# Stage two of a graph kernel: ten blocks gathered at its beginning in place of three, then four blocks of adds with no gather between them

## What is computed

```python
h = relu(layernorm(x))
# layer 0: messages go from dst to src
gate = silu(edge_attr @ W1.T + b1) @ W2.T + b2 + adapt_logit(types of src and dst)
msg  = gate * h[dst] * (cutoff(distance) * mult[dst])
agg  = segment_sum(msg, src) / clip(segment_sum(mult[dst], src), 1e-8)
x    = x + layernorm(h + agg) * gamma + beta
# layer 1: messages go from src to dst
h    = relu(layernorm(x))
msg  = (relu(h @ weight1 + bias1) @ weight2)[src, rel_type] * norm
x    = x + relu(segment_sum(msg, dst) + bias2)
```

## Time and profile before

| | |
|---|---|
| time, median of 3 executions | 1542.93 us (1542.01 to 1545.06) |
| the profiled execution | 1533.91 us |
| its span, first to last instruction | 1532.2 us |
| busy: PE, DVE, ACT, POOL | 1157.1, 1336.7, 618.2, 1025.5 us |
| mean granted TensorE clock | 0.598 of full speed |

### The profile page before, as it was taken

How to read it: one execution, slowest core, us unless ns; L and a number is a source line. 1 busy time by engine, 2 the same in 40 slices (tenths; PEclk the granted TensorE clock), 3 DMA queues, 4 the chain that set the end, 5 groups by cost and what they waited for, 6 DMA issues and landing times.

```text
span 1532.2 us, 20105 instructions
## 1 busy us (share of the span) xinstructions
PE 1157.1 (76%) x5198; PEld 846.7 (55%) x5198; DVE 1336.7 (87%) x3937; ACT 618.2 (40%) x1423; POOL 1025.5 (67%) x809
## 2 busy tenths in 40 slices
PE   5898999989999989991047878888888888886000
PEld 2677777777777777771035555555555555554000
DVE  6999999999999999880299999999999999993598
ACT  2544444544445444440034444444444444442000
POOL 7655567777887676666537887887878878866100
PEclk9756555655556565555556565555655655557555
DMA  7999986666666566642446665555555555533899
GB/s 228 305 320 333 325 228 155 153 145 145 142 164 154 136 155 138 147 103 11 130 156 169 170 161 139 140 139 140 138 137 139 140 141 139 140 71 58 295 396 390
DMA packets 154389, 268.72 MB, mean 175 GB/s; under 512 B 73818, under 2 KB 90411, under 8 KB 153380
## 3 DMA queue, kind: packets, MB, share of 16 engines
q1 hardware_dynamic: 78228, 223.53, 43.5%
q0 software_dynamic: 68992, 24.64, 17.5%
q10 hardware_dynamic: 7056, 19.27, 3.1%
HBM read 194.33 MB, written 112.55 MB: 200 GB/s over the span
## 4 chain that ended last, share of the span: by engine, by line
PE 32%; DMA 20%; DVE 19%; POOL 15%; issue 11%; ACT 3%; SPq 1%; POOLq 0%; ACTq 0%; DVEq 0%
POOL agg L468 11%; PE ps_m L555 11%; DMA t<-agg,src_all 6%; PE ps_m L644 6%; PE ps_qs L555 4%; DMA agg<-x,once 3%; PE ps_k L630 3%; DMA lows<-low 2%; DVE x L1038 2%; DVE same L834 2%; DMA agg<-y,once 2%; DVE t L1042 2%; POOL nodes L426 2%; DMA agg<-ysq,once 2%; POOL agg L504 2%
## 5 line engine op out<-in xcount | busy, mean ns | idle before, releaser
L504 POOL DMA_INDIRECT agg<-sums,once x196 | 317.8, 1621 | 89.5 <-issue 64.1
L426 POOL DMA_INDIRECT nodes<-in_table,dst_all x196 | 194.1, 990 | 104.0 <-issue 50.2
L495 POOL DMA_INDIRECT t<-agg,src_all x196 | 190.3, 971 | 83.7 <-issue 49.1
L555 PEld LDWEIGHTS ps_m<-msg,same 128*128 128x128 f32 x980 | 200.4, 314 | 29.8 <-issue 29.8
L555 PE MATMUL ps_m<-msg,same 128*128 128x48 f32 x980 | 208.2, 398 | 1.0 <-issue 1.0
L630 PE MATMUL ps_k<-h_t,rw_sb 56*128 56x256 f32 x588 | 132.3, 571 | 96.3 <-ACT hid L724 73.7
L555 PEld LDWEIGHTS ps_qs<-msg,same 128*128 128x128 f32 x980 | 183.0, 288 | 2.1 <-DVE msg L926 2.1
L555 PE MATMUL ps_qs<-msg,same 128*128 128x49 f32 x980 | 180.1, 362 | 2.0 <-DVE msg L926 2.0
L468 POOL DMA_INDIRECT agg<-x,once x84 | 135.1, 1609 | 49.0 <-issue 21.9
L630 PEld LDWEIGHTS ps_k<-h_t,rw_sb 56*128 56x128 f32 x588 | 67.6, 260 | 144.6 <-ACT hid L724 100.6
L644 PE MATMUL ps_m<-hid,rw_sb 128*64 128x256 f32 x588 | 136.1, 634 | 0.0
(11 more groups left out here) (149 smaller groups left out, 2575.1 us busy)
## 6 DMA issues: line engine op xcount, KB each, us to landing
agg<-in_both SPq DMA_DIRECT2D x14, 2758.0 KB
t<-agg SPq DMA_DIRECT2D x49, 784.0 KB, 4.4
kept<-kept_out SPq DMA_DIRECT2D x49, 404.0 KB, 2.8
kept_in<-kept SPq DMA_DIRECT2D x49, 404.0 KB
agg<-bias_rows SPq DMA_DIRECT2D x49, 384.0 KB
out<-t ACTq DMA_DIRECT2D x49, 384.0 KB, 5.8
rows<-in_src_rows SPq DMA_DIRECT2D x49, 256.0 KB, 4.1
rows<-in_dst_rows SPq DMA_DIRECT2D x49, 256.0 KB, 3.2
```

The lines of the kernel that those rows point to most:

```text
L426: pool.indirect_dma_start(nodes[s][:, t, :], None, table, bass.IndirectOffsetOnAxis(ap=dst_all[:, c:c + 1], axis=0)).then_inc(nodes_in[b % ...
L495: pool.indirect_dma_start(t2[b % T2S][:, t, :], None, wide, bass.IndirectOffsetOnAxis(ap=src_all[:, c:c + 1], axis=0)).then_inc(ends_in[b ...
L504: pool.indirect_dma_start(agg1, bass.IndirectOffsetOnAxis(ap=once1[b % LAG1][:, t:t + 1], axis=0), sums1[b % LAG1][:, t, :], None, compute ...
L555: last = mm(ps[:, t * width:(t + 1) * width], kept_same[:, at:at + P], m[:, v, :], start=(v == t), stop=(v == TILES - 1))
```

## The change

A second kind of slot is made: `t2_early`, seven of them (`EXTRA` = `PRE1` - `T2S` = 10 - 3), lies in the beginning of `x_res`. Blocks 0 to 6 use these; block b from 7 on uses `t2[(b - 7) % 3]`. The semaphores `chunk_in` and `ends_in` become rings of ten. GpSimd gathers blocks 0 to 9 first, with no wait for an `x2_done` between them; the loop after them gathers block b + 6 only where that is 10 or more, so that the adds of blocks 0 to 3 stand alone. SP still loads chunks three blocks ahead. Both SP and GpSimd now wait for `agg1_set` before they write into slots, since the fills read `bias_rows`, which lies in the memory that `x_res` takes over; GpSimd had this wait ahead of its first add.

```diff
+PRE1 = 10
+EXTRA = PRE1 - T2S
...
+        x_flat = x_res[:, :, :].rearrange("p r h -> p (r h)")
+        t2_early = [x_flat[:, k * G * XW:(k + 1) * G * XW].rearrange("p (r w) -> p r w", w=XW) for k in range(EXTRA)]
+        def t2_slot(b):
+            return b if b < EXTRA else EXTRA + (b - EXTRA) % T2S
+        def t2_uses(b):
+            return 1 if b < EXTRA else (b - EXTRA) // T2S + 1
+        def t2_of(b):
+            return t2_early[b] if b < EXTRA else t2[(b - EXTRA) % T2S]
...
-        chunk_in = ring_of(sem, T2S, "chunk_in")
-        ends_in = ring_of(sem, T2S, "ends_in")
+        chunk_in = ring_of(sem, PRE1, "chunk_in")
+        ends_in = ring_of(sem, PRE1, "ends_in")
...
+            sp.wait_ge(S["agg1_set"], 16 * (NBLOCK + 1))
...
-                if t == 0:
+                if t == 0 and b >= PRE1:
                     need(pool, S["x2_done"], b - T2S + 1)
...
-            for b in range(AHEAD1):
+            pool.wait_ge(S["agg1_set"], 16 * (NBLOCK + 1))
+            for b in range(PRE1):
                 for t in range(TILES):
                     gather_wide(b, t)
-            pool.wait_ge(S["agg1_set"], 16 * (NBLOCK + 1))
             for b in range(NBLOCK):
                 for t in range(TILES):
                     add1(b, t)
-                if b + AHEAD1 < NBLOCK:
+                if PRE1 <= b + AHEAD1 < NBLOCK:
                     for t in range(TILES):
                         gather_wide(b + AHEAD1, t)
```

More of the change, by code:

```diff
@@ L215, in build @@
         x_res = sb("x_res", [P, RES * NR + TILES, H])
+        x_flat = x_res[:, :, :].rearrange("p r h -> p (r h)")
+        t2_early = [x_flat[:, k * G * XW:(k + 1) * G * XW].rearrange("p (r w) -> p r w", w=XW) for k in range(EXTRA)]
+        assert EXTRA * G * XW <= (NBLOCK - PRE1 - T2S) * NR * H
+        def t2_slot(b):
[4 more added lines that the diff above has]
+            return t2_early[b] if b < EXTRA else t2[(b - EXTRA) % T2S]
         def x_rows(b):
@@ L371, in load_chunk @@
                 need(sp, S["x2_done"], b - T2S + 1)
-                sp.dma_start(t2[s][:, TILES:G, :].rearrange("p r w -> p (r w)"), wide_chunks[b]).then_inc(chunk_in[s], 16)
+                sp.dma_start(t2_of(b)[:, TILES:G, :].rearrange("p r w -> p (r w)"), wide_chunks[b]).then_inc(chunk_in[t2_slot(b)], 16)
                 sp.dma_start(kept_in[s][:, TILES * H:TILES * H + KEPT], kept[b]).then_inc(kept_got[s], 16)
@@ L492, in gather_wide @@
                 c = b * TILES + t
-                if t == 0:
+                if t == 0 and b >= PRE1:
                     need(pool, S["x2_done"], b - T2S + 1)
-                pool.indirect_dma_start(t2[b % T2S][:, t, :], None, wide,
-                                        bass.IndirectOffsetOnAxis(ap=src_all[:, c:c + 1], axis=0)).then_inc(ends_in[b % T2S], 16)
+                pool.indirect_dma_start(t2_of(b)[:, t, :], None, wide,
+                                        bass.IndirectOffsetOnAxis(ap=src_all[:, c:c + 1], axis=0)).then_inc(ends_in[t2_slot(b)], 16)
             def add1(b, t):
@@ L933, in _ @@
                 yes = 0 <= b < NBLOCK
-                on = t2[b % T2S]
-                on_a = t2[a % T2S]
+                on = t2_of(b) if yes else None
+                on_a = t2_of(a) if a < NBLOCK else None
                 kin = kept_in[b % T2S]
@@ L938, in _ @@
                 if yes:
-                    dve.wait_ge(chunk_in[b % T2S], 16 * uses(b, T2S))
+                    dve.wait_ge(chunk_in[t2_slot(b)], 16 * t2_uses(b))
                     V.tensor_scalar(tot[:, :], on[:, :, XW - 1:XW].rearrange("p r o -> p (r o)"), 1e-8, None, ALU.max).then_inc(S["tot_done"], 1)
                 if a < NBLOCK:
-                    dve.wait_ge(ends_in[a % T2S], 16 * TILES * uses(a, T2S))
+                    dve.wait_ge(ends_in[t2_slot(a)], 16 * TILES * t2_uses(a))
                     V.tensor_reduce(asum[:, :], on_a[:, 0:TILES, 0:H], AX_X, ALU.add).then_inc(S["asum_done"], 1)
```

## The result

The changed kernel is slower. Its median is **1556.62 us** (1553.38 to 1559.27, 5 executions) beside 1542.93 us (1535.13 to 1546.87, 5) of the kernel before: a ratio of **1.0089**, 95% interval 1.0055 to 1.0123. Forecast were 1539.9 us and a range from 1536.0 to 1543.0, so the time lies outside it, on the other side of no change.

The account below looks back on a forecast made before the run. Stage two was taken as bound by a loop of copy, adds, gathers and `asum`, 26.00 us per two blocks. The only gain, 3.06 us at block 10, gave 1542.93 - 3.06 = 1539.9 us, range 1536.0 to 1543.0.

Parts of the forecast that it names:

- Forty gathers in a run: Start of stage two on POOL: 28 more gathers at 1.25 us end 9.7 us before the first add, costing nothing.
- Contention: Early stage two: extra gathers start after the first chunks land and delay only small later traffic with room; no cost.
- The stall of block 6: Stage two, block 6: its gathers land early, so `asum` no longer waits and comes 2.30 us earlier.
- Passes with adds alone: Stage two, blocks 7 to 9: gathers already in, 12.46 us per VectorE pass; lead grows to 3.06 us.
- Rival 2: Adds hold VectorE's `tot` in four free passes, 0.29 us each; gain only 1.9 us, 1541.0 us; chance 14%.
- What is late next: Block 10's gathers stand behind block 4's adds: `asum` waits about 1.1 us, yet comes 3.06 us earlier than before.
- The 16 gathers taken out of the loop: Blocks 6 to 9: POOL is spared 20.0 us, mostly not gained because adds wait for ScalarE's copies.
- the end of stage two: VectorE's schedule, not POOL's backlog, sets the end, so the 3.06 us lead reaches stage three whole.
- Rival 3: POOL alone is the limit in stage two: up to 20 us gained, 1522.9 us, or 1536 in small form; chance 8%.
- Waits on `agg1_set`: Before slot writes: fills issued 70 us earlier, so the waits are met and cost under 0.1 us each.
- Rival 4: POOL's queue stalls the forty gathers, each further one waiting for the previous landing: 11 us later, 1553.9 us; chance 6%.
- The bound of 0.2%: Whole kernel: 3.1 us taken as the smallest difference a measurement can tell from no change; forecast gain almost exactly there.

Follow-up runs that it names:

- e5: Kernel with the change but six blocks gathered early, plus 16 gathers nobody reads, so again forty in a run: 1551.87 us, ratio 1.0075 to the kernel before.
- e6: Kernel with the change but six blocks gathered early, plus 16 POOL memsets in place of further gathers: 1547.71 us, ratio 1.0023 to the kernel before.
- e7: Kernel before with gathers of block b + 6 put ahead of adds of block b in stage two's loop: 1527.82 us, ratio 0.9909.
- e9: Changed kernel with a small POOL memset, waited for, behind each of the 28 further gathers: 1530.24 us, ratio 0.9984 to the kernel before.
- e1: Kernel before, unchanged, run again for a second trace: 1543.80 us, a single execution.
- e8: Kernel before with two blocks instead of four gathered ahead at the start of stage one: 1535.45 us, ratio 0.9968.
- e3: Changed kernel with eight blocks gathered ahead instead of ten, a run of 32 gathers: 1549.91 us, ratio 1.0044 to the kernel before.
- e12: Changed kernel with further gathers paced by VectorE's progress, gathers ahead of adds, and two first blocks in stage one: 1518.58 us, ratio 0.9913 to the kernel before.
- e4: Changed kernel where, from block 3, a block's early gathers wait until those of the block before have landed: 1549.20 us, ratio 1.0051 to the kernel before.

## Why the prediction was wrong

- *Forty gathers in a run*: **the step that failed.** Its sum was right as far as it went. The run took 1.25 us each and lasted 50.4 us, from 753.18 to 803.60; without stage one's loss it would have ended at 794.3, and 793.7 were forecast. But "costs nothing" looked only at when POOL is wanted next. The price was on the engines beside it: 15.4 us in the changed kernel's trace. That the run of gathers makes it is shown by e5, which has the run but not the order of the change, against e6. It is not paid everywhere: nothing like it is in the traces of the third chip, where the changed kernel itself was not run.
- *Contention* failed with it. It counted bytes and the DMA engines' time, and there it was right: their share was 0.55 and not higher. The delay is not there.
- *The stall of block 6*: right. No wait of `asum` between blocks 2 and 9.
- *Passes with adds alone*: right, 12.46 to 12.60 us where 12.46 were forecast. *Rival 2* is in the difference: `tot` took 0.44 us at 841.12 and 853.72, and both passes took 12.60. It had 0.29 us for each of four passes; 0.14 in two of them was measured. The same mechanism, and not POOL's backlog, is most of what e7 has left above 12.46 us.
- *What is late next*: right in size, 3.06 us. The changed kernel gained 3.7 us after its stall and e9 3.6, or 2.6 each if e1 stands for the kernel before. Only the wait of 1.1 us at block 10 was not seen: its `asum` followed 12.52 us after that of block 9 in the changed kernel.
- *The 16 gathers taken out of the loop* and *the end of stage two*: right, the pace of later passes did not improve (13.03 against 12.97). *Rival 3* did not occur. The adds of block 44 were to start at about 1372. They started at 1398.21, again after a wait of 6.51 us for ScalarE's copy as in the earlier trace rows, so VectorE's schedule set the end, only 23.2 us later, carried from the two places above.
- *Waits on `agg1_set`*: right. The first gather waited 2.0 us for the last add of stage one, as before (1.99 us in the earlier trace rows).
- *Rival 4* had the right sign, the right part of the change and nearly the right size (11 us; 11.7 at block 10 by the traces), but another mechanism: a gather that waits for the one before it. POOL's pace never changed. What I held against it, was read one-sidedly: 32 gathers 1.30 us apart say that POOL can issue them so, and nothing of what the other engines do meanwhile. That execution showed no loss there, and the next one of the same kernel did (e1); the second condition was met in the one and not in the other. A question to one execution can't show what only some have; the 9 us between its time and the median were the hint, and I moved them over as a constant.
- *The bound of 0.2%* was too fine: with five executions of each kernel the interval of the ratio is 0.34% wide to either side, so that a gain of 3.06 us could not have been told from none.

**What stays open.** Which resource delays the others is not known. It is not the DMA engines' share (0.55, like before) and not POOL's being busy (e6). It is hardly the loading of instructions, with one packet of 0.02 MB for it between 778 and 803 us of the changed kernel, and two with as much in the same stretch of before. Most of the late starts are late semaphore updates, as shown above, but not all: `DVE_READ_ACCUMULATOR`, which waits for no semaphore and otherwise starts without a pause, started 0.42 us late at 805.72. Nor is the second condition known. All timed executions are recorded, and it is the record itself that has holes where losses occur. Between 778 and 808 us of the changed kernel 51 updates were due: 2 are recorded in time, 12 late and 37 not at all. So the recording, or whatever both share, is a rival that no run here excludes: it may be that the records and the gathers get in each other's way, and that the stall is smaller or absent in an execution that is not recorded. Holes alone don't stall, since they go on after 850 us, where the passes are 13.0 us. For stage one the cause was not separated: e8 breaks the run and gathers the first blocks later at once, so that it is only argued that the run is what costs there.

## What to carry to other kernels

Before gathering far ahead, ask what a long dense run does to the engines beside it: on two of the three chips it cost more than early gathers could win. Whether a small space between gathers cures it is worth a run, on a chip that shows the loss; here it was tried only on one that did not. Where adds that must wait for another engine stand ahead of gathers that needn't, exchange them first: two lines were worth 14 us, and the extra slots nothing on top. When the profiled execution lies far from the median, take a second one before using it to rule anything out. And run a cure on the chip that has the illness, beside the kernel that it is to cure: a ratio to the kernel before doesn't make up for a chip on which the loss never occurs.

## What the runs showed that was not expected

- On chips 4 and 15, and in the first trace of the changed kernel, a run of indirect gathers 1.25 us apart, each 128 rows of 98 floats, makes VectorE, ScalarE and TensorE start late: 1.4 us are lost with 24 in a row, 8.3 with 32 and 15.4 with 40 (e6, whose memsets may have a part in it, e3, and the changed kernel). It begins after about 25 gathers and ends some microseconds after the run. The waits are ended by "remote" or "issue", up to 2.35 us each on VectorE in stage two, and the semaphore updates behind them are up to 3.7 us late. On chip 9 no such loss is seen: not beside 32 gathers 1.30 us apart in stage one of e9, nor beside e12's runs of 8, 8 and 12.
- An indirect DMA that waits for the landing of the one before stood 1.8 to 5.8 us in e4; the long ones fall beside the chunk loads (the one of 5.80 us ends at 823.25, and a chunk was issued at 815.91).
- `tot` was held beside an add for 0.44 us in place of 0.17, but a pass lengthened by 0.14 us only. Nearly all held ones end 1.03 to 1.07 us after the start of the add's issue on POOL, which itself takes 1.54 us or more.
